# An attention layer with routed experts on one core: masked copy of the decayed product behind both normalisations, thirteen result buffers in place of five

## The reference

```python
q, k, v = x @ Wq, x @ Wk, x @ Wv            # 16 query heads, 4 key/value heads, 128 wide
g = k                                       # gates: log_sigmoid(g) / 16
qs, ks = softmax(q, -1), softmax(k, -1)
S_t = S_{t-1} * exp(g_t) + ks_t v_t^T       # linear attention with decay
o_gla_t = qs_t S_t
y = softmax(causal(rope(q) rope(k)^T / sqrt(128))) @ v
x1 = layernorm(x + (0.5 * y + 0.5 * o_gla) @ Wo)
w = softmax(x1 @ gate_w.T); top 2 of 8 experts for each token
out = layernorm(x1 + sum over both experts of w_e * (silu(x1 @ w_gate_e) * (x1 @ w_up_e)) @ w_down_e)
```

## Time and profile before

| | |
|---|---|
| median of 3 executions | 942.73 us (941.15 to 943.13) |
| the profiled execution, its own time | 952.46 us |
| its span, first to last instruction | 950.7 us |
| mean granted TensorE clock (share of full speed) | 0.985 |
| busy, share of the span: PE, PEld | 95%, 75% |
| DVE, ACT, POOL | 71%, 70%, 67% |
| attention steps, routing within them | 18 to 820 us |
| experts | 820 to 931 us |
| weighing, second LayerNorm, output | 924 to 951 us |

### The profile page before, as it was taken

How to read it: one execution, slowest core, us unless ns; L and a number is a source line. 1 busy time by engine, 2 the same in 40 slices (tenths; PEclk the granted TensorE clock), 3 DMA queues, 4 the chain that set the end, 5 groups by cost and what they waited for, 6 DMA issues and landing times.

```text
span 950.7 us, 18329 instructions
## 1 busy us (share of the span) xinstructions
PE 907.8 (95%) x5145; PEld 714.4 (75%) x5145; DVE 675.1 (71%) x2010; ACT 662.2 (70%) x2147; POOL 635.6 (67%) x603
## 2 busy tenths in 40 slices
PE   7899999999999999999999999999999998888996
PEld 4677777777777777777777787787777766677895
DVE  4786877676767676767676969786887867573457
ACT  6677777777777777777676868677776766344656
POOL 6868686767565657777686757777676888444341
PEclk9899999999999999999999999999999999798999
DMA  7101100000000000700000001001002111133346
GB/s 261 34 12 29 29 24 1 6 13 7 1 0 0 0 0 7 212 24 1 1 2 1 1 1 43 1 2 32 1 17 104 61 39 57 52 111 101 108 139 210
DMA packets 30970, 41.48 MB, mean 44 GB/s; under 512 B 3230, under 2 KB 25631, under 8 KB 30624
## 3 DMA queue, kind: packets, MB, share of 16 engines
q1 hardware_dynamic: 27472, 31.98, 11.1%
q0 software_dynamic: 3408, 8.43, 2.5%
HBM read 24.72 MB, written 16.59 MB: 43 GB/s over the span
## 4 chain that ended last, share of the span: by engine, by line
PE 74%; DVE 11%; ACT 4%; issue 4%; POOL 3%; DMA 2%; another core or an unknown queue 1%; POOLq 0%; SPq 0%; DVEq 0%; ACTq 0%
PE PR L518 11%; PE OA L631 11%; PE S L585 9%; PE MS L604 8%; PE S L613 7%; PE OA L593 4%; PE S L731 4%; PE OA L624 3%; PE OA L748 3%; PE PR L558 3%; PE PR L564 3%; ACT eqk L879 2%; DVE S L1077 2%; POOL slot_x L1720 1%; DMA acc<-in_x_rows 1%
## 5 line engine op out<-in xcount | busy, mean ns | idle before, releaser
L1647 POOL TENSOR_TENSOR qd<-eqk,eg 128x512 f32<-128x512 f32 x63 | 74.9, 1189 | 142.6 <-issue 137.2
L631 PE MATMUL OA<-wT,V 128*128 128x512 f32 x320 | 149.8, 599 | 0.0
L841 ACT ACTIVATE S<-S,nm 128x128 f32<-128x128 f32 (+3 forms) x256 | 126.7, 495 | 9.6 <-DVE nm L1077 8.9
L1077 DVE CUSTOM_DVE_ANT_0 S<-S,maskb 128x128 f32<-128x128 f32 (+3 forms) x256 | 118.3, 518 | 16.1 <-PE S L585 12.3
L879 ACT ACTIVATE eqk<-qkv,nmx 128x128 f32<-128x128 f32 x320 | 124.3, 396 | 4.0 <-DVE nmx L1152 3.9
L1635 POOL TENSOR_TENSOR eqk<-eqk,rse 128x640 f32<-128x640 f32 x63 | 79.6, 1263 | 57.7 <-DVE rse L1195 37.0
L631 PEld LDWEIGHTS OA<-wT,V 128*128 128x128 f32 x320 | 60.2, 192 | 70.0 <-issue 70.0
L1111 DVE TENSOR_TENSOR pr<-S,rl 128x256 f32<-128x256 f32 (+3 forms) x128 | 105.6, 825 | 4.5
L1624 POOL TENSOR_TENSOR rp<-qkv,cos 128x640 f32<-128x640 f32 x64 | 99.6, 1557 | 6.7 <-ACT qkv L869 6.7
L1627 POOL TENSOR_TENSOR rp<-rp,rt 128x640 f32<-128x640 f32 x64 | 99.8, 1559 | 5.0
L604 PE MATMUL MS<-wo,oT_hi 128*128 128x256 f32 (+1 forms) x512 | 97.6, 289 | 4.1 <-DVE gc L1120 1.9
(11 more groups left out here) (251 smaller groups left out, 2460.6 us busy)
## 6 DMA issues: line engine op xcount, KB each, us to landing
qkv<-slot_x SPq DMA_DIRECT2D x39, 129.0 KB
slot_x<-zero SPq DMA_DIRECT2D x3, 1290.0 KB, 14.5
stage<-in_wgu SPq DMA_DIRECT2D x8, 352.0 KB, 3.2
stage<-in_wqkv SPq DMA_DIRECT2D x6, 384.0 KB, 3.6
xraw<-in_x_cols SPq DMA_DIRECT2D x16, 128.0 KB, 2.4
acc<-in_x_rows SPq DMA_DIRECT2D x1, 2048.0 KB, 11.6
dn_w<-in_wdn SPq DMA_DIRECT2D x1, 2048.0 KB, 8.0
pr<-plane SPq DMA_DIRECT2D x8, 256.0 KB, 2.9
```

Source lines behind the costliest of these rows:

```text
L631: last = pe.matmul(OA[:, :], V[:, j, :], wT[:, j, :], start=(c == 0 and j == 0), stop=(j == c))
L841: nc.scalar.activation(S[:, h, 0:n], S[:, h, 0:n], ACT.Exp, bias=nm[:, h:h + 1], scale=-1.0, accum_out=ls[:, h:h + 1]).then_inc(s_exp, 1)
L1077: nc.vector.tensor_tensor_reduce(out=S[:, h, 0:n], in0=S[:, h, 0:n], in1=maskb[:, N - n:N], scale=-1.0, scalar=FAR, op0=ALU.add, op1=ALU.m ...
```

## The change

Two edits. `mask_gla` stood ahead of the first `normalise` in steps with c = 1, 2, 3 and behind the second with c = 0; it now stands behind the second in all. `YO` goes from 5 to 13: the five buffers in `eqk` stay, and two more each lie in `V`, `x1T`, `rt` and `rqT`, which the attention stage has left by then.

```diff
-YO = 5
+YO = 13
...
-        yo = eqkf[:, 0:YO * HID].rearrange("p (a n) -> p a n", a=YO)
+        yo = [x[:, i * HID:(i + 1) * HID] for x, n in ((eqkf, 5), (V[:, :, :].rearrange("p a b -> p (a b)"), 2), (x1T, 2), (rt, 2), (rqT, 2)) for i in range(n)]
...
-                nc.scalar.copy(yo[:, q % YO, :], OA[:, 0:HID]).then_inc(s_yo, 1)
+                nc.scalar.copy(yo[q % YO], OA[:, 0:HID]).then_inc(s_yo, 1)
...
                 if c == 1:
                     feature_sums(g, c + 1)
-                if c:
-                    mask_gla(g, c)
                 clamp_first = c in (1, 2)
                 if n1 and clamp_first:
                     clamp_gates(g, c + 1)
...
                 if n1 and not clamp_first:
                     clamp_gates(g, c + 1)
                 normalise(g, c, 1)
-                if c == 0:
-                    mask_gla(g, c)
+                mask_gla(g, c)
...
-                                             yo[:, q % YO, :], None, bounds_check=2 * B * N - 1, oob_is_err=False).then_inc(s_y[q % YO], 16)
+                                             yo[q % YO], None, bounds_check=2 * B * N - 1, oob_is_err=False).then_inc(s_y[q % YO], 16)
```

## The result

The changed kernel takes 936.34 us (median of 4 runs, 935.75 to 937.13), the kernel before on the same chip 942.93 (941.15 to 943.30): ratio 0.9934, 95% interval 0.9917 to 0.9952, so 6.2 us less by the ratio, between 4.5 and 7.8 (6.6 by the medians). The forecast was 935.9. The profiled execution of the change took 935.75 us with a span of 933.5.

What follows compares the result with a forecast made beforehand. TensorE was taken to bound the kernel, its waits read from start to start. From the median 942.73, the mask's 5.9 us (2.9 + 2.95) and the buffers' 0.9 gave 935.9 us, range 933.8 to 939.8.

Steps and rivals of the forecast that it cites:

- What bounds, and how to read it: Attention steps run back to back on TensorE; idle column gives about 2 us, gaps read start to start give 5.9.
- The term of c = 3: L604 waits for the gate-sum copy: 0.10 us in eleven steps, 1.15, plus 1.8 from three large waits; 2.95 us.
- The term of c = 2: L613 waits for the second `pr`; the whole wait goes in 14 steps between 43 and 700 us, 2.9 us.
- c = 1 at nothing: Moving the mask's 0.61 us costs nothing; covered by 0.37 before `KT_hi` and 1.23 between `rq_lo` and the scores.
- Rival (c): Slower through c = 1: the moved mask delays `rq_lo` and the scores, up to 9.8 us in 16 steps, 945.7; chance 0.03.
- Nothing behind 729 us: Gains in attention steps after 729 us not counted, since GpSimd's sends and weight splits run to the experts' stage.
- The buffers at 0.9 us: Thirteen buffers spare y_out(12) its wait for send_back(7), some 1.5 us; taken as 0.9, bounds 0 and 1.5.
- up to 0.5 of the 1.5 is given back: Tile 17's slot load, ready at 862.5 for a transpose due at 862.0, takes back part of the buffers' gain.
- The stall: y_out(8) starts at 853.95, not 850.9, in the profiled execution before; taken to belong to that execution alone.
- Rival (d): The stall is in every execution and is a lack of buffers; some 10 us go as well, 925.9; chance 0.05.
- (a): Closed gaps are given back at TensorE's next wait: half of 5.9, nothing from the buffers, 940.2; chance 0.13.
- (b): Nothing moves: 0.1 us gaps are the sequencer's own and five buffers are enough, 942.2, within 0.2%; chance 0.05.

Runs made afterwards that it cites:

- c = 3 alone: Kernel before with five buffers, mask moved behind both normalisations only in steps with c = 3: 938.61 us, ratio 0.9965.
- c = 2 alone: Kernel before with five buffers, mask moved behind both normalisations only in steps with c = 2: 939.72 us, ratio 0.9978.
- experiment 4: The change, with the mask ahead again in the one c = 2 step that has routing work before the sum of outputs: 936.34 us, ratio 0.9941.
- the later sends: The change, with the eight sends of the last tokens behind send_back(7) instead of ahead of it: 939.45 us, ratio 0.9973.
- one more copy: The change, with the masked copy made twice behind the normalisations in steps with c = 1: 938.49 us, ratio 0.9967.

## Why the prediction was right, point by point

**What bounds, and how to read it.** Right. TensorE is busy for 498 of 500 us before and after, and the steps were shortened by 0.44 us in four. The idle column would have given 2 us; starts gave 5.9, and the mask alone measured 5.9 (0.0063 of 942.2; 4.6 to 7.2). That the two figures are the same is luck, as the next two terms show.

**The term of c = 3, 2.95 us: too small, it measured 4.1 in the steps.** (By its time, c = 3 alone gave 3.3, 2.0 to 4.6, which would not tell the two apart.) Three large waits of 0.6 were 0.51, 0.51 and 0.73. The eleven small ones were 0.22 each and not 0.10. The step that failed is "single matmuls compared, it is 0.10 us": the distance from L518 to L604 shows only half of the wait, and the other half stands inside the pair of L604 that follows, 0.51 us in the earlier trace rows where the same pair with c = 0 in the same group has 0.40. The row was there, and I read its start and not its length.

**The term of c = 2, 2.9 us: too large, it measured 0.8 to 1.5 in the steps.** (By its time, c = 2 alone gave 2.1, 1.2 to 2.9.) The same mistake made ten steps too small (0.16 in the step shown, where 0.22 came). But "if ScalarE's exponentials are done, and they are in c = 2 and 3" is false in steps 2, 6, 50 and 54, on which 1.2 of the 2.9 rested: VectorE waits there for ScalarE instead. And step 54 lost 0.75 of its own, where the routing work between `pr` and the sum of outputs, with the mask now ahead of it, ran into a longer product of GpSimd's and made L568 wait by 0.55. The two errors, 1.2 too little and some 1.9 too much in the change, have opposite signs, and steps 53 and 56 gained what had not been counted (0.33 and 0.36); so the sum over the steps is 5.7, and 5.9 came out by luck.

**c = 1 at nothing: right, by the wrong cover.** Alone the run was 0.8 us slower (0.0 to 1.7), of which the steps show 0.1 outside step 42, and nothing is seen in the pair of the change and its c = 1 undone. I set 0.37 + 1.23 us against it, up to the scores. The nearest customer of what is behind the mask is not the scores but L568, which waits for the sum of outputs, and what it had left after the move is 0.83 us in the step shown and 0.07 in step 33. With the 0.61 that was moved the cover was 1.44 and 0.68, where I had 1.60. Rival (c) had the mechanism and the wrong place, and in step 33 it was 0.07 us away.

**Nothing behind 729 us, because GpSimd's chain takes over.** Nothing came behind step 56, as forecast: steps 57, 59 and 61 of the change are 0.33, 0.20 and 0.34 us shorter than with thirteen buffers alone, but 58, 60 and 62 are 0.33, 0.24 and 0.19 longer. TensorE's first slot transpose comes 6.7 us earlier in the change (806.40 against 813.12): 5.7 come between steps 3 and 56, and 1.0 before step 3, where executions differ by as much. That it is GpSimd's chain that takes over was not tested by itself; putting step 54 right gives back most of its gain in steps 55 and 56, already ahead of 729.

**The buffers at 0.9 us: mis-sized, no gain is seen.** The wait of y_out(12) is real (2.0 us late with five). What failed is "up to 0.5 of the 1.5 is given back": by the traces all of it is, to within their spread. I put tile 17's slot load at 862.5 for a transpose due at 862.0, with 2.4 us for the last send to land; in the change the send takes 4.38 from issue and TensorE stands for 1.89. The seven results from y_out(7) to y_out(14) take 18.1 us on average in six profiles with thirteen buffers (17.45, 17.48, 17.96, 18.31, 18.54 and 18.67) and 18.3 in four with five (17.85, 18.40, 18.42 and 18.46); in those six the last send's landing took anything from 3.75 to 4.47 us, where I had 2.4. The bound of 0 was the value, or close to it.

**The stall.** Rival (d) is out: in the four profiles of other kernels with five buffers y_out(8) follows y_out(7) by 2.26 or 2.27 us. It belonged to that one execution, and what it was stays open.

**Rivals (a) and (b).** (a) is out, since the forecast's distances came and the next step is no longer; (b) is out by the 0.20 to 0.24 us per ordinary step. Two sums in the prediction don't come out: half of 5.9 is 2.95, so (a) stands at 939.8 and not 940.2, and the three large waits with half of the small ones are 1.8 + 2.0 = 3.8, where the low end says 3. The measured 936.34 lies inside either way.

## What to carry to other kernels

Read a wait from start to start and then go on to the length of the next group, against the same group where nothing waits: half of a short wait can hide in it. When something is moved behind an instruction, list every customer of what now comes later and take the nearest, not the one that the kernel's story is about. And when a wait is removed, look at what is due within the same microsecond: here a wait of 1.7 us was removed and another of 1.9 stood behind it. Last, a forecast that comes out is no proof of its terms: here two of them were off by a microsecond or more, in opposite directions, and only the lengths of the steps told.

## What was not expected of the hardware

**VectorE beside GpSimd.** A small product of two SBUF operands takes 0.33 us or 1.43, and both times it ends 0.11 or 0.12 us after the GpSimd product during which it began, one of 0.51 us or one of 1.60. The Trainium skill has this as a lock (SBUF — State Buffer, SBUF: two separate sides): a VectorE instruction with two SBUF inputs and a GpSimd one that reads SBUF share a pair of ports, and whichever starts second is blocked for the whole of the first. The rows of experiment 4 agree. The mask itself reads PSUM and took 0.68 us in either place, but moving it moved what came after into GpSimd's way.

**TensorE's clock after a pause.** Pauses of 2.49, 2.55 and 4.76 us in the experts' stage were followed by 3.4 to 4.6 us of work at half the clock, those of 1.30 + 0.59 and 1.41 + 0.31 by none. With 2.49 and 2.55 the fall shows only some 1.4 us after TensorE is back at work; with 4.76 it comes during the pause. So the wait cost twice: 2.5 us of pause took another 1.4 to 1.6. Counting the wait alone gave 0.9 to 1.3 for the later sends, and 3.1 was measured. The length of the pause does not settle it, though. Late in the attention stage TensorE waits 2.38 us for GpSimd in the change and with one more copy alike (L565 is L564 there); first the change, with the granted clock behind it, then the other:

```profile
766.31 0.66 PE L564 MATMUL PR<-cm,qd 128*128 128x128 f32 x4 [2.38 <-POOL qd L1648]
```

```profile
767.00:772.00 5.00, 4.80 (x26) 1.00 0.02 5
```

```profile
768.40 0.66 PE L565 MATMUL PR<-cm,qd 128*128 128x128 f32 x4 [2.38 <-POOL qd L1655]
```

```profile
770.00:772.00 2.00, 2.00 (x8) 0.50 0.03 8
```

The first stays at full clock and the second falls to half. What decides between them these runs don't show.
